# A six-block decoder kernel on one core: attention and choice split into stations of two halves, banks handed over per product

## The reference, cut to what matters

```python
# x: (32, 128, 256); ctx: (32, 128, 256); mask: (128, 128)
x = layernorm(x + windowed(x))       # 16 heads of 16, window of 7 neighbours, softmax times `conn`, renormalised
x = layernorm(x + cross(x, ctx))     # one head of 256, softmax(q k^T / 16 + mask) v
x = layernorm(x + experts(x))        # 8 experts, each the top 16 tokens of a sequence by sigmoid logits, rope, attention
x = layernorm(x + decayed(x))        # one head, scores times gamma ** distance
x = layernorm(x + memory(x, ctx))    # argmax over scores picks one context row per token; 16-head attention over the picks
x = layernorm(x + feed_forward(x))   # activations to 8 bits by row, weights to -1/0/1, conv of 3, silu, 8 bits again

# windowed:
attn = softmax(scores); fw = attn * conn; fw = fw / (fw.sum(-1) + 1e-9); out = einsum(fw, Vw) @ wo.T + bo
# feed_forward:
act_quant(x) = clip(round(x * scale), -128, 127) / scale,  scale = 127 / max(|x|)
weight_quant(w) = clip(round(w / mean(|w|)), -1, 1) * mean(|w|)
```

## Time and profile before

| | us |
|---|---|
| median of 3 runs | 1100.07 (1093.01 to 1100.21) |
| the profiled execution | 1096.73 |
| its span, first to last instruction | 1094.9 |
| TensorE, VectorE, ScalarE, GpSimd busy | 964.1, 910.3, 752.5, 163.2 |
| mean granted clock of TensorE, share of full speed | 0.947 |

### The profile page before, as it was taken

The page is one execution under the profiler, slowest core; times in us unless marked ns, Lnnn a source line. Parts: engine busy times, 40 slices in busy tenths (PEclk is TensorE's granted clock), DMA queues, the critical chain, the costliest instruction groups (busy, mean ns, idle before and its releaser), DMA issues.

```text
span 1094.9 us, 19705 instructions
## 1 busy us (share of the span) xinstructions
PE 964.1 (88%) x7038; PEld 693.7 (63%) x7038; DVE 910.3 (83%) x2503; ACT 752.5 (69%) x1854; POOL 163.2 (15%) x401
## 2 busy tenths in 40 slices
PE   5758889999999999999999999999999998887552
PEld 4536557676767676767767776768676756564331
DVE  4798776689898989898989989898999877867754
ACT  2223454768696878778787878786969795867643
POOL 2000110111112020302021211112120301010000
PEclk9878899999999999999999999999999998988865
DMA  7823021211110302030303020120212001000000
GB/s 224 325 67 106 1 87 34 63 46 42 49 58 9 98 21 86 6 101 1 106 1 90 17 81 26 45 63 20 77 40 68 10 1 30 1 20 1 10 10 10
DMA packets 36626, 58.90 MB, mean 54 GB/s; under 512 B 6784, under 2 KB 15872, under 8 KB 36016
## 3 DMA queue, kind: packets, MB, share of 16 engines
q1 hardware_dynamic: 36528, 57.64, 16.7%
HBM read 28.65 MB, written 4.19 MB: 30 GB/s over the span
## 4 chain that ended last, share of the span: by engine, by line
PE 68%; ACT 14%; DVE 12%; POOL 3%; issue 3%; DMA 0%; SPq 0%; ACTq 0%; POOLq 0%; DVEq 0%
PE bank_c L450 20%; PE bank_a L450 11%; PE banks_e L450 7%; PE bank_f L450 5%; PE bank_x L450 5%; PE bank_x L644 4%; PE bank_a L542 3%; PE bank_c L472 2%; ACT squares_out L1362 2%; ACT area_e L1559 2%; DVE x L880 2%; DVE area_a L1046 2%; PE banks_e L788 1%; PE banks_e L801 1%; ACT area_bx L1350 1%
## 5 line engine op out<-in xcount | busy, mean ns | idle before, releaser
L1284 DVE SCALAR_TENSOR_TENSOR area_f<-area_f,w_convw 128x254 f32<-128x254 f32 x256 | 111.5, 477 | 6.0 <-ACT area_f L1588 4.9
L1350 ACT ACTIVATE area_bx<-bank_x 128x512 f32<-128x512 f32 (+1 forms) x144 | 70.0, 498 | 29.3 <-PE bank_x L644 10.4
L1208 DVE TENSOR_REDUCE neg_top<-banks_e 128x8 f32<-128x1024 f32 x64 | 76.1, 1211 | 10.4 <-PE banks_e L450 10.3
L996 DVE TENSOR_TENSOR area_a<-area_a 128x512 f32<-128x512 f32 x112 | 73.4, 681 | 8.6 <-ACT area_a L1350 8.5
L1588 ACT ACTIVATE area_f<-area_f,w_convb,w_convw 128x256 f32<-128x256 f32 x128 | 69.6, 594 | 13.7 <-DVE area_f L1275 13.6
L1350 ACT ACTIVATE area_a<-bank_a 128x512 f32<-128x512 f32 (+1 forms) x80 | 44.1, 551 | 49.9 <-PE bank_a L450 28.3
L1350 ACT ACTIVATE area_bx<-bank_c 128x512 f32<-128x512 f32 x64 | 34.8, 544 | 61.3 <-PE bank_c L450 41.3
L1046 DVE TENSOR_TENSOR area_a<-area_a 128x512 f32<-128x512 f32 x112 | 74.4, 681 | 0.4
L1559 ACT ACTIVATE area_e<-banks_e 128x512 f32<-128x512 f32 x128 | 67.9, 599 | 1.3 <-PE banks_e L801 1.0
L1050 DVE TENSOR_TENSOR area_a<-area_a 128x512 f32<-128x512 f32 x96 | 65.1, 679 | 0.1
L1350 ACT ACTIVATE area_e<-banks_e 128x512 f32<-128x512 f32 (+1 forms) x80 | 45.8, 593 | 16.1 <-PE banks_e L472 5.9
(11 more groups left out here) (314 smaller groups left out, 2682.7 us busy)
## 6 DMA issues: line engine op xcount, KB each, us to landing
area_a<-area_a SPq DMA_DIRECT2D x96, 224.0 KB
area_a<-in_xT SPq DMA_DIRECT2D x16, 256.0 KB, 2.9
x<-in_x SPq DMA_DIRECT2D x16, 256.0 KB, 3.0
area_bx<-in_ctxT SPq DMA_DIRECT2D x16, 256.0 KB, 2.8
area_d<-in_ctxT SPq DMA_DIRECT2D x16, 256.0 KB, 3.0
y<-x SPq DMA_DIRECT2D x16, 256.0 KB, 2.2
w_wqkv_e<-in_wqkv_e SPq DMA_DIRECT2D x1, 3072.0 KB, 10.5
area_f<-in_raw SPq DMA_DIRECT2D x2, 1024.0 KB, 11.4
```

The source lines that it names most:

```text
L996: return dve.tensor_tensor(product_of(wi).rearrange("p (n t) -> p n t", t=P), qT0.rearrange("p c (b t) -> p (c b) t", t=P), kT0.rearrange( ...
L1208: dve.tensor_reduce(top[:, b, :, r:r + 2, 0].rearrange("p (par c) r -> p r c par", c=DC), banks_e[:, r:r + 2, :].rearrange("p r (c par k) ...
L1284: last = dve.scalar_tensor_tensor(c4[:, i, :, dst], h4[:, i, :, src], cwt3[:, 2 * jj + i, k:k + 1], c4[:, i, :, dst], ALU.mult, ALU.add)
L1350: return act.activation(dst, src, ACT.Copy)
```

## The change

Stations: A loses its first part to a new station Q `queries` (load of xT, q, k and v products and copies, the first `EARLY = 4` of the seven q*k products, the shifts), and the choice becomes a station of its own, D. Q of the next group waits only for what it overwrites: `a_heads` for q and k, `a_values` for v. Area D gets its own `xT_d` and `o_d`; A's last copy gets its own `oT0`.

Banks: `BANK_TURNS` and `turn_in_c` go. TensorE keeps a dictionary `held` from bank to the semaphore of the last reader: `take(bank)` waits for it ahead of each product in banks a and c, `until` sets it after.

TensorE: biases and offset are 128 rows deep (zero rows beside the three). `neg_top` holds all parts in one block of 128 columns: 2 transposes, one copy of 256 columns; the product that spreads them takes constant weights `quarters` and is 16 matmuls of 128 columns per sequence, in place of 4 of 512. The sums over w2 are taken on VectorE.

VectorE: one sum fewer in the window softmax (`conn_more = conn + 1e-9`); the router's reciprocal is a flip of bits with a reciprocal of 16 values later; E's two products per sequence are one; fewer small steps at F's scales; the setup yields at nearly each instruction. To ScalarE go the rounding of the weights (Copy with `MAGIC`, then Sign, `SLICES = 4`, mean by Abs with a sum), the rounding of x in F and the chosen keys. The order strings of all engines are new (TensorE 952 letters).

```diff
-SLICES = 8
+EARLY = 4
+
+SLICES = 4
...
-BANK_TURNS = "BBB" + (NG - 3) * "CB" + "CCC"
...
-        "AAAAASASSSSBBAAAABSABAABABBXXAASXBAAXAXBAXBAAXXBBXXXXBSXABXXAASXBAXAXBXABBXAXCACXXXCXCXCCXACACXCACXACXCA"
+        "QQQASSAASSSQBQBAADQSABBAASBBQBQXXBAAXSQXXABXBAAXBXQBXXBXXQXABAXCXQAXBXBXBABXACQXCXQXCXXXCAXCAXBXQAXDDXDX"
...
-                    row = slice(32 * bias, 32 * bias + 3)
-                    pe.matmul(bank[:, :], ones_bf[row, :], bc(bias_parts[row, :], 1, GB), start=True, stop=False)
+                    pe.matmul(bank[:, :], ones_bf[:, :], bc(bias_parts[bias][:, :], 1, GB), start=True, stop=False)
...
+            held = {}
+
+            def take(bank):
+
+                if bank in held:
+                    pe.wait_ge(*held[bank])
+
+            def until(bank, read, count):
+
+                held[bank] = read, count
...
+            def queries(g):
                 pe.wait_ge(xt_in, 16 * (g + 1))
                 if g:
-                    pe.wait_ge(n_a.added, g)
+                    pe.wait_ge(a_heads, 2 * g)
...
+                take("a")
+                project(bank_a, chunked("wq0"), xT0).then_inc(a_qk_proj, 1)
+                until("a", a_qk, 2 * g + 1)
+                yield
...
+                if g:
+                    pe.wait_ge(a_values, g)
+                take("a")
+                project_rows(bank_a, chunked("wv0"), xT0).then_inc(a_v_proj, 1)
+                until("a", a_v, g + 1)
+                yield
...
-                turn_in_c("B", g)
+                take("c")
                 project(bank_b, w_cross, blocks(ctxT_b)).then_inc(b_proj, 1)
-                yield
-                pe.wait_ge(b_kav, 2 * g + 1)
+                until("c", b_kav, 2 * g + 1)
+                yield
...
-                turn_in_c("C", g)
                 pe.wait_ge(n_x.done, g + 1)
+                take("c")
                 to_channels(bank_c, xs[g % NX]).then_inc(c_xT, 1)
+                until("c", c_xT_out, g + 1)
...
                 pe.wait_ge(ctxd_in, 16 * (g + 1))
-                pe.wait_ge(n_c.added, g + 1)
+                take("c")
...
-                    for at in range(4):
-                        last = pe.transpose(bank_e[b][:, at * P:(at + 1) * P], neg_top[:, b, at, :], I)
+                    last = pe.transpose(bank_e[0][:, b * P:(b + 1) * P], neg_top[:, b, :], I)
...
-                    for r in range(4):
-                        pe.matmul(bank_e[r][:, :], ones_bf[group[r], :], negT_e[group[r], b * 4 * P:(b + 1) * 4 * P],
-                                  start=True, stop=False)
+                    for a in range(4):
+                        for r in range(4):
+                            pe.matmul(bank_e[r][:, a * P:(a + 1) * P], quarters[group[r], a, :],
+                                      negT_e[group[r], b * P:(b + 1) * P], start=a == 0, stop=False)
...
-                m = own.mark(dve.reciprocal(sig, sig))
+                m = own.mark(dve.tensor_scalar(r2.bitcast(U32), sig.bitcast(U32), 0x7FFFFFFF, None, ALU.bitwise_xor))
...
-                key = chosen_key[g % 2]
-                dve.tensor_tensor(key[:, 0], bc(bank_c[:, 0:P], 1, 2), bc(w["parity"][:, :], 2, P), ALU.mult)
-                dve.tensor_tensor(key[:, 1], bc(bank_c[:, P:2 * P], 1, 2), bc(w["parity"][:, :], 2, P),
-                                  ALU.mult).then_inc(d_key_out, 1)
...
+                for par in range(2):
+                    act.activation(chosen_key[i][:, :, par, :], blocks(bank_c[:, 0:T], GB), ACT.Copy,
+                                   scale=w["parity"][:, par:par + 1])
+                    yield
...
-                for b in range(GB):
-                    last = copy(negT_e[:, b * 4 * P:(b + 1) * 4 * P], bank_e[b][:, :])
-                last.then_inc(e_negT_out, 1)
+                copy(negT_e, bank_e[0][:, 0:T]).then_inc(e_negT_out, 1)
...
+                act.wait_ge(f_scaled, 2 * g + 1)
+                for b in range(GB):
+                    last = act.activation(xq_f[:, b * D:(b + 1) * D], xs[g % NX][:, b, :], ACT.Copy, scale=sc1_f[:, b:b + 1], bias=MAGIC)
+                last.then_inc(f_quantized, 1)
+                yield
...
-                copy(xqT_f, bank_f[:, :]).then_inc(f_xqT_out, 1)
+                act.activation(xqT_f, bank_f[:, :], ACT.Copy, bias=-MAGIC).then_inc(f_xqT_out, 1)
...
+                    act.activation(q, raw, ACT.Abs, accum_out=small[:, i:i + 1]).then_inc(setup_act, 1)
+                    yield
...
+                            made[k] = own.mark(act.activation(part, part, ACT.Copy, scale=small[:, 2 + i:3 + i], bias=MAGIC))
+                            yield
+                        if k:
+                            act.wait_ge(own.sem, made[k - 1])
+                            last = act.activation(q[:, (k - 1) * n:k * n], raw[:, (k - 1) * n:k * n], ACT.Sign,
+                                                  bias=less_magic)
```

More of the change, by code:

```diff
@@ L80 @@
[L80 to L89, removed]
@@ L427, in cross, with choose @@
                 yield
-            def decayed(g):
+            def choose(g):
                 if g:
@@ L557, in windowed @@
                 last.then_inc(a_values, 1)
+                until("a", a_oT, g + 1)
                 yield
-                pe.wait_ge(a_oT, g + 1)
                 if g == 0:
                     pe.wait_ge(setup_dve, 6)
-                project_rows(bank_a, chunked("wo0"), qT0, 0).then_inc(a_wo, 1)
+                take("a")
+                project_rows(bank_a, chunked("wo0"), oT0, 0).then_inc(a_wo, 1)
+                until("a", n_a.added, g + 1)
                 yield
-            def turn_in_c(station, g):
-                before = [i for i, name in enumerate(BANK_TURNS) if name == station][g] - 1
-                if before >= 0:
-                    groups = BANK_TURNS[:before + 1].count(BANK_TURNS[before])
-                    if BANK_TURNS[before] == "B":
-                        pe.wait_ge(n_b.added, groups)
-                    else:
-                        pe.wait_ge(d_v_out, groups)
             def cross(g):
@@ L722, in decayed @@
                 last.then_inc(c_pv, 1)
+                until("c", n_c.added, g + 1)
                 yield
-                yield from choose(g)
             def choose(g):
@@ L892, in split_bias @@
                     m = own.mark(dve.tensor_tensor(rest, rest, bias_round[r, :], ALU.subtract))
+                yield
                 dve.wait_ge(own.sem, m)
-                return dve.tensor_copy(parts, part)
+                dve.wait_ge(setup_pool, 12)
+                for at in range(r.start, r.stop, 32):
+                    last = dve.tensor_copy(bias_parts[at // 32][at:at + 32, :], bias_rest[at:at + 32, :])
+                last.then_inc(setup_dve, 1)
+                yield
             def setup(_):
@@ L988, in setup @@
-                    if i:
-                        last.then_inc(setup_dve, 1)
+                    dve.reciprocal(small[:, 2 + i:3 + i], wmean[:, i:i + 1]).then_inc(setup_dve, 1)
+                    yield
+                dve.wait_ge(setup_act, 12)
+                m = own.mark(dve.tensor_reduce(bias_rest, w2q[:, :, :].rearrange("p j n -> p n j"), X, ALU.add))
+                yield
+                dve.wait_ge(own.sem, m)
+                dve.tensor_copy(w2_sums[:, :], bias_rest).then_inc(setup_dve, 1)
@@ L1428, in windowed @@
                 act.wait_ge(a_values, g + 1)
-                copy(qT0, blocks(bank_a[:, :])).then_inc(a_oT, 1)
+                copy(oT0, blocks(bank_a[:, :])).then_inc(a_oT, 1)
                 yield
```

437 lines of the change are left out of this document (233 added, 204 removed).

## The result

The kernel after takes 1086.2 us (median of 7 runs, 1079.4 to 1089.9) against 1098.5 us for the kernel before, run on the same chips (7 runs, 1093.0 to 1100.2): a ratio of 0.989, 95% interval 0.985 to 0.992. It is faster, by 12.3 us where 39.5 were forecast. The profiled execution took 1083.2 us, 1081.4 of it span.

A forecast was written before the change was run, and what follows sets the result against it. It took TensorE and VectorE, both 92% used and waiting for each other in written-out order, as the bound; 11.0 + 10.5 - 7 + 16 + 6 + 3 = 39.5 us off 1096.7 gave 1057 us, range 1028 to 1088.

The forecast's parts named there:

- Tile sizes: TensorE: 117 fewer changes of tile size, mostly from 128-row biases and offset, at 0.094 us each: 11.0 us saved.
- Transposes: TensorE: neg_top transposes fall from 8 to 2 a group, 96 fewer at 0.11 us each: 10.5 us saved.
- quarters: TensorE: 16 products of 128 columns per sequence replace 4 of 512, costing 0.46 us a group, 7 us in all.
- The third rival: Slower: the 128-column products load weights openly, one after another, 57 us more than forecast, 1114 us; chance 0.05.
- The waits at bank_c: Middle: the new order covers TensorE's waits between steps of C and D, net 1.0 us a group, 16 us saved.
- VectorE to ScalarE: VectorE has 3.4 us less a group, ScalarE 0.9 more; not on the path by itself, value 0.
- The head: First 125 us: weight quantization moves from VectorE to ScalarE; 6 of the 17 us credited.
- The end: Last group's chain loses a reciprocal, time in F's two scale chains and a copy: 3 us saved.
- the first: Rival: only engine work counts, waits wander elsewhere and the head is set by its chain; 1079 us, chance 0.22.
- The fourth: Rival: new order's waits land behind ScalarE, 1.3 us a group lost, no head gain; 1100 us or slightly below; chance 0.08.
- The second: Rival: the two full engines pushed each other and VectorE's relief frees them, 45 us instead of 16; 1028 us, chance 0.15.
- The mark set for a wrong forecast: Middle: a group at 57.5 us with waits in bank_c for oT's copy or in F for quantized x.

The follow-up runs named there:

- b_tiles: Kernel before with only the bias and offset products made 128 rows deep, old order; 1088.9 us, 0.989 of before.
- b_q: Kernel before with only the once-turned table (fewer neg_top transposes) and the quarters products, old order; 1095.9 us, 0.997 of before.
- b_all: Kernel before with all edits to a group's work, but the old order, old bank turns and old setup; 1082.9 us, 0.987 of before.
- a_turns: Kernel of a_sp with a searched order, turns at bank_a and bank_c kept as in the kernel after; 1036.0 us, 0.943 of before.
- b_dve: Kernel before with only the edits to VectorE's and ScalarE's work, old order and banks; 1101.0 us, 1.004 of before.
- b_pe: Kernel before with only TensorE's edits (128-row biases and offset, once-turned table with quarters), old order and banks; 1083.9 us, 0.987 of before.
- a_sp: Kernel after with transposed-x loads issued before the preceding group's shifts, and group 0's shifts before the large weight loads; 1077.5 us, 0.981 of before.
- a_ord: Kernel of a_sp with only the order of steps changed, by swapping neighbours while a trace replay got shorter; 1034.1 us, 0.941 of before.

## Why the prediction was right in sign and wrong in size

- **Tile sizes, 11.0 us:** right. 101 of the 117 changes gave 9.8 us in b_tiles, 9.5 by the prediction's 0.094 each. (Counted in the traces by rows and columns of up to 32, 64 or 128, b_tiles has 106 changes fewer and the kernel after 114; that gives 0.092 each.)
- **Transposes 10.5, quarters -7, net 3.5 us:** b_q measured 2.7, so the net was right, with some luck. By starts the transposes are 0.22 us a group in place of 0.87, 10.4 us in all, as counted. The step with 16 quarter products and the eight score sets behind them takes 1.25 us instead of 1.19: 0.12 us a group, 2 us in all, not 7. The third rival (57 us more) is refuted by L831: 512 of them in 13.1 us, against 12.8 for the 128 they replace. But of the work that b_q saves by starts, 0.44 us a group or 7 us, well under half came off the time, and that makes up for the quarters' error; with the tile edit beside it the two gave 14.7 us together.
- **The waits at bank_c, 1.0 us a group, 16 us: the step that failed.** The prediction counted the work put between consecutive steps of C and D and took the covered waits as gone, with one new wait against them. By starts the four covered waits fell from 1.5 us a group to 0.7; one of them, the choice's query product, waits longer than before (0.33 against 0.16). The new wait, at the choice's last product, is 0.4 where 0.5 was priced. So the turn of C and D gave 0.5 us a group and not 1.0. What the prediction didn't count at all is the other stations. The order of 61 steps on TensorE beside some hundred on VectorE was written anew, and E, X, B, A and F wait 1.6 us a group more together, E's last projection alone 0.4. Waiting is 5.8 us a group against 4.7: 1.1 worse, not 1.0 better. Against b_all, which has the same work, the new order's shortest distances add up to 0.6 less; half of that is the head sums named above, which in the old order were 0.3 longer in every group. Together the middle lost 0.4 us a group to the new order (57.6 against 57.2). It was a count over some steps of one engine where the whole order had to be replayed. The prediction's own remark that the bank still passes in whole turns was right but for 7 breaks, and a_turns shows that the turns are not the point.
- **VectorE to ScalarE, 0:** right (b_dve 2.4 us slower, b_all 1.0 us faster than b_pe). By busy time VectorE lost 1.6 us a group in the middle where 3.4 were counted, but the count was right: the durations of its records there add up to 60.2 us a group instead of 63.8, 3.6 less. Busy time is the union of records that overlap, and they overlap less now.
- **The head, 6 us:** wrong, and not for the reason weighed. VectorE does have 80.9 us in the first 125 in place of 92.8, ScalarE 53.1 in place of 39.0. The prediction wrote of SyncE's queue only that a wait disappears ahead of the shifts. It missed that the new order issues the expert weights ahead of group 0's shifts and group 1's load, so that this load lands 12.9 us after its issue instead of 2.8: a_sp, with the weights behind and each load ahead of the shifts, has 8.6 us less. What the quantization of the weights on ScalarE gave by itself was not tried.
- **The end, 3 us:** from group 14's `wo0` bias to the end of TensorE's last record, 277.4 us against 285.7, so 8 came; 3 of them are in b_all too.

Of the rivals the first (only engine work counts, the waits wander) had the mechanism, and 1079 us would have been nearly the time but for the late loads: a_sp has 1077.5. That it comes so near is partly luck, since its sum has 3 us for the end where 8 came and nothing for the waiting added in the middle. The fourth named places where waits arose (D's last step, the copies of the choice), but putting x's quantization back on VectorE did not make it faster. The second, both full engines freed, is refuted: VectorE got its relief and waited 20 us longer for TensorE at one line. The mark set for a wrong forecast was met: "a group at 57.5 with waits in bank_c for oT's copy".

The rule of the Trainium skill that was weighed against the quarters ("TensorE: Matmul & The Clock Gate", "LDWEIGHTS (loading the stationary operand)" and "The mechanism") would have made them cost 14 us by the prediction's estimate, and b_q 3.5 us slower than before; b_q, 2.7 us faster, and 0.12 us a group by starts speak against it for 128-column products in four row groups.

Left open: why VectorE's edits cost 0.4% alone; which swaps of the searched order bring its 43 us, above all the 17 to 20 ahead of group 6; which of a_sp's two edits its gain is from; and whether the weight quantization on ScalarE helps.

## What to carry to other kernels

Where engines run in a written-out order, price work and waiting apart: here work taken off the fullest engine came off, and the waiting stayed with the order. A new order can't be judged by the waits that it covers; replay it with the durations and hand-overs of a trace, all engines together, its head and end included, and count what it newly makes late. And list what a moved DMA now stands behind: 4 MB issued ahead of a small load held it back by 10 us, though SyncE issued it hardly later.

## What the runs showed of the hardware that was not expected

- Sixteen 32x128 bf16 products, each with weights to load, in four row groups, begin at 474.03, and what follows them at 474.27, 0.24 us later. Four 32x512 products take 0.23. The 16 loads of weights (PEld) begin within the same 0.23 us: for so short a stream they are still hidden.

```profile
474.03 0.40 PE L831 MATMUL banks_e<-area_e,w_quarters 32*128 32x128 bf16 x16
474.27 1.09 PE L835 MATMUL banks_e<-chosen_q,chosen_key 32*128 32x256 f32 x16
```

```profile
474.03 0.23 PEld L831 LDWEIGHTS banks_e<-area_e,w_quarters 32*128 32x128 bf16 x16 [0.62 <-issue]
```

- A 128-row product with 125 rows of zeros is cheaper here than the 3-row one: both stream 512 columns, and the next product starts 0.22 us after it instead of 0.31. b_tiles gives 0.09 to 0.10 us for each change of tile size.
- The twelve DMAs of group 0's shifts hold SyncE's queue for 8.7 us (9.6 in a_sp), 0.7 to 0.8 us each on average, where the two loads of expert weights take 0.43 each.
- A load of 256 KB took 12.9 us from issue to landing behind 4 MB of weights, 2.8 us without them.
- The same instructions in another order take 4% less time: 1034 us in a_ord against 1077.5 in a_sp.
